# Idle products ahead of the input's transposes, and one query projection moved between the two products of a linear attention

## The chip, the cores and the metric

The kernel runs on one core of a Trainium2 chip. The metric is the device time of one execution in microseconds (us), lower is better. Engines are named as the profile names them: PE is TensorE's matmul side and PEld its weight loads, DVE is VectorE, ACT is ScalarE, POOL is GpSimd, SP is SyncE, whose queue issues most loads.

## The reference

One graph layer over N = 384 nodes with D = 1024 features, everything in float32:

```
xn = layernorm(x)
x  = x + gnn(xn) + mix(xn)
x  = x + moe(layernorm(x))

gnn: q, k, v = xn Wq, xn Wk, xn Wv (+ biases); q2, k2, v2 = q Wiq, k Wik, v Wiv
     16 heads of softmax(q2 k2^T / 8 + edge mask) v2, then Wo
mix: q, k, v = xn Wqkv + b; qp, kp = elu(q) + 1, elu(k) + 1
     attn = qp (kp^T v) / (qp sum(kp) + 1e-6)
     x1 = layernorm(xn + attn); layernorm(x1 + (silu(x1 Wg) * (x1 Wu)) Wd)
moe: 8 experts, each row through the one that its logits pick
```

The change touches the layer norm and transposes at the very start, the linear attention of mix, and the first query projection of gnn.

## The kernel before

The program is written by hand, an instruction stream for each engine, tied by semaphores. Nothing is scheduled by a tool: each engine does its work in the order in which its block of the source has it. Each product in full precision is made of three passes over a high and a low part of both factors (`PASSES`), so every operand has a high half, made by ACT as a rounded copy, and a low half, made by DVE as the difference (`lo`).

**Weights.** They come from one stream of 512 KB quarters. SP loads a quarter into one of four slots of `raw`, ACT rounds it into `wsp` (`prep`, profile line 664), DVE subtracts (`prep`, shown as line 977), and PE takes the quarter (`open_quarter` waits for `w_lo`). The engines stay two quarters ahead. `feature_major` (line 1625) makes one 128-row block of a projection from a quarter: 24 matmuls of 128x384 into PSUM bank 0 or 1, which alternate. `open_acc` makes PE wait until the block before the last has left its bank; `acc_part` (ACT line 671, then DVE line 988) empties a bank into the high and low half of a block of features.

**Start.** SP loads x in three tiles of 128 rows. DVE takes statistics (lines 994 and 996), POOL the reciprocal root (529, 530), DVE scales the tile (1009, `xn_done`). PE transposes each tile in eight blocks (1654), ACT copies them out (679), DVE makes the low half. Then come the quarters of mix's q and k with their elu (lines 695 to 710 on ACT, 1071 on DVE), then v in token order (1639).

**Linear attention.** It is computed as (qp kp^T) v rather than qp (kp^T v). The first product, line 1690, makes three blocks of 384x384 scores from `feat[2]` (keys) and `feat[1]` (queries), evacuated by `acc_part` into `pt`. PE then waits until the last of them is out (`acc_free`), and for each tile of rows makes the denominators (1704, six matmuls of two columns) and the second product (1709, eighteen matmuls of 128x512) into banks 2 to 7. DVE divides, adds and takes statistics for each tile (1134 to 1139).

```
            pe.wait_ge(acc_free, acc.value)
            pe.wait_ge(tm_lo, 2 * NT)
```

**Projections of gnn.** Three loops of two turns with four quarters each follow on PE (line 1715): eight blocks of q into `feat[1]`, eight of k, eight of v. ACT and DVE have matching loops. Between DVE's steps of the query projections stand pieces 12 to 15 of the edge code search (`piece`, line 1053), 10 and 11 stand between the tiles of the linear attention. POOL makes the codes for each piece (lines 556, 558) and then writes edges to DRAM one column at a time (573). SP loads the rows for pieces 10 to 15 between the quarters 24 to 32.

Of the kernel before, what the change touches and what calls it, by code (L numbers as in the profile page):

```python
# [25 lines left out]
P = 128  # L26
# [3 lines left out]
KT = D // P  # L30
# [5 lines left out]
GROUP = 3  # L36
# [10 lines left out]
RING = 4  # L47
# [6 lines left out]
B_MQ, B_MK, B_Q, B_K, B_V, B_IQ, B_IK, B_IV, B_G, B_U = 0, 8, 16, 24, 32, 40, 48, 56, 64, 67  # L54
# [47 lines left out]
@contextmanager  # L102
def repeat(engine, times, per):

    first = {t: t.n for t in per}
    with engine.Fori(0, times) as i:
        for t, n in per.items():
            t.i, t.per = i, n
        yield i
    for t, n in per.items():  # L110
        assert t.n == first[t] + n, (t.n, first[t], n)
        t.n, t.i = first[t] + n * times, None
# [38 lines left out]
def graph_layer(nc, x, rowb, cols, consts, later, src_rows, dst_rows, src_cols, dst_cols, type_cols,  # L151
                type_weights, w_stream, w_experts, switch_w, b12, out):
    with ExitStack() as ctx:
        def sb(name, shape, dt=F32):
            return ctx.enter_context(nc.sbuf_tensor(name, shape, dt))

        def sem(name):
            return ctx.enter_context(nc.semaphore(name))
# [16 lines left out]
        feat = [b[:].rearrange("p h (k n) -> p h k n", k=KT) for b in bigs]  # L175
# [23 lines left out]
        row_buf = sb("row_buf", [P, D])  # L199
# [4 lines left out]
        bias = sb("bias", [P, NBIAS])  # L204
# [6 lines left out]
        with nc.sbuf_tensor("low_rows", [P, N], F32) as low_rows:  # L211
# [42 lines left out]
        junk, late_junk = ([work[:, b * N:(b + 1) * N], work[:, (b + 1) * N:(b + 2) * N - P],  # L254
                            work[:, (b + 2) * N - P:(b + 2) * N]] for b in (2, 4))
# [20 lines left out]
        ps = ctx.enter_context(nc.psum_tensor("ps", [P, 8, HALF], F32))  # L276
# [3 lines left out]
        ys_dram = nc.dram_tensor("slot_y", [SLOTS * SLOT, D], F32).ap()  # L280


        x_in = [sem(f"x_in{t}") for t in range(NT)]
        ident_set, const_in, edge_in, rowb_in, b_row_in, route_in = (
            sem("ident_set"), sem("const_in"), sem("edge_in"), sem("rowb_in"), sem("b_row_in"), sem("route_in"))
# [5 lines left out]
        acc_ready, acc_hi, acc_free = sem("acc_ready"), sem("acc_hi"), sem("acc_free")  # L291
# [360 lines left out]
        def _(act):  # L652
            q_no = Tally()
            used = [Tally() for _ in range(XRING)]
            acc = Tally()
            everyone = slice(0, P)

            def prep(slot):


                act.wait_ge(raw_in[slot], used[slot].add(16))
                if q_no.i is not None or q_no.n >= RING:
                    act.wait_ge(w_started, q_no.value - 1)
                nc.scalar.activation(wsp[:, 0, slot, :], raw[:, slot, :], ACT.Copy).then_inc(w_hi, 1)  # L664
                q_no.add()

            def acc_part(dst, rows, b):

                bank = acc.n % 2
                act.wait_ge(acc_ready, acc.add())  # L670
                nc.scalar.activation(dst, ps[rows, bank, 0:N], ACT.Identity, bias=b).then_inc(acc_hi, 1)  # L671

            turn = {q_no: RING, acc: RING, **{u: 16 for u in used[:RING]}}
# [59 lines left out]
                acc_part(pt[:, 0, mt, :], everyone, 0.0)  # L733


            for n, b0 in enumerate((B_Q, B_K, B_V)):
                with repeat(act, 2, turn) as i:
                    for j in range(RING):
                        m = i * RING + j
                        acc_part(feat[1 + n][:, 0, bass.ds(m, 1), :], everyone, bias[:, bass.ds(m + b0, 1)])  # L740
                        prep((j + 2) % RING)
# [223 lines left out]
        def _(dve):  # L965
            q_no, step = Tally(), Tally()
            acc, hi_no = Tally(), Tally()
            everyone = slice(0, P)
# [10 lines left out]
            def prep(slot):  # L979
                dve.wait_ge(w_hi, q_no.add())  # L980
                lo(wsp[:, 1, slot, :], raw[:, slot, :], wsp[:, 0, slot, :]).then_inc(w_lo, 1)

            def acc_part(dst, hi, rows, b):

                bank = acc.n % 2
                acc.add()
                dve.wait_ge(acc_hi, hi_no.add())
                nc.vector.scalar_tensor_tensor(out=dst, in0=ps[rows, bank, 0:N], scalar=b, in1=hi.bitcast(F32),  # L988
                                               op0=ALU.add, op1=ALU.subtract).then_inc(acc_free, 1)
# [8 lines left out]

            turn = {q_no: RING, acc: RING, hi_no: RING}

            nc.vector.memset(ones_r[:].bitcast(F32), 1.0).then_inc(ones_set, 1)
            for t in range(NT + 1):
                if t < NT:
# [43 lines left out]
            parts, elus, pieces, edges = Tally(), Tally(), Tally(), Tally()  # L1047

            def piece(buf, c, into):

                dve.wait_ge(codes_done, pieces.value + 1)
                for k in range(GROUP):
                    ins = nc.vector.scalar_tensor_tensor(  # L1053
                        out=into[k], in0=codes[buf][:, k * P:N], scalar=ef[:, 0, bass.ds(c + k, 1)],
                        in1=maskb[:, k, k * P:N], op0=ALU.is_equal, op1=ALU.mult,
                        accum_out=dup[:, bass.ds(c + k, 1)])
                ins.then_inc(piece_done, 1)
                dve.wait_ge(piece_done, pieces.add())
                cs = bass.ds(c, GROUP)
                then(nc.vector.scalar_tensor_tensor(out=ef[:, 1, cs], in0=dup[:, cs], scalar=0.0, in1=ef[:, 2, cs],  # L1060
                                                    op0=ALU.is_gt, op1=ALU.mult))
                nc.vector.tensor_tensor(eidx[:, cs], ef[:, 1, cs], ef[:, 0, cs], ALU.add).then_inc(edges_done, 1)
                edges.add()
# [43 lines left out]
            for h in range(2):  # L1107
                for j in range(RING):
                    prep((j + 2) % RING)
                    if j % 2:  # L1110
                        n = 6 + 2 * h + j // 2
# [9 lines left out]
                for t in range(NT):  # L1121
# [2 lines left out]
                    lo(tokv[3][:, 1, t, cols_h], work[:, t * HALF:(t + 1) * HALF], tokv[3][:, 0, t, cols_h])\  # L1124
                        .then_inc(tm_lo, 1)

            for mt in range(NT):
                acc_part(pt[:, 1, mt, :], pt[:, 0, mt, :], everyone, 0.0)


            for t in range(NT):
# [7 lines left out]
                statistics(t)  # L1139
                if t < 2:  # L1140
                    piece(t, (10 + t) * GROUP, late_junk)

            def projection(n, m, j, b0):

                acc_part(feat[1 + n][:, 1, bass.ds(m, 1), :], feat[1 + n][:, 0, bass.ds(m, 1), :],
                         everyone, bias[:, bass.ds(m + b0, 1)])
                prep((j + 2) % RING)

            def x1_scaled(t):

# [9 lines left out]
                nc.vector.scalar_tensor_tensor(out=row, in0=row, scalar=rs[:, t, 1:2], in1=rowbuf[:, 1, :],  # L1160
                                               op0=ALU.mult, op1=ALU.add).then_inc(x1_done, 1)

            with repeat(dve, 2, {**turn, pieces: 2, edges: 2, step: 2}) as i:
                for j in range(RING):
                    projection(0, i * RING + j, j, B_Q)
                    if j % 2:
                        piece(j // 2, i * (2 * GROUP) + (12 + j // 2) * GROUP, late_junk)
            with repeat(dve, 2, turn) as i:
                for j in range(RING):
                    projection(1, i * RING + j, j, B_K)  # L1170
# [431 lines left out]
        def _(pe):  # L1602
            q_no, acc = Tally(), Tally()

            def open_quarter():

                pe.wait_ge(w_lo, q_no.add())
# [9 lines left out]
            def feature_major(slot, moving, between=None, after=3):  # L1617

                open_quarter()
                bank = open_acc()  # L1620
                for k in range(KT):
                    if between and k == after:
                        between()
                    for n, (a, b) in enumerate(PASSES):
                        ins = nc.tensor.matmul(ps[:, bank, 0:N], wsp[:, a, slot, k * P:(k + 1) * P],  # L1625
                                               moving[:, b, k, :], start=(k == 0 and n == 0),
                                               stop=(k == KT - 1 and n == 2))
                        if k == 0 and n == 0:
                            ins.then_inc(w_started, 1)
                ins.then_inc(acc_ready, 1)  # L1630
# [15 lines left out]

            turn = {q_no: RING, acc: RING}

            pe.wait_ge(ident_set, 1)

            for t in range(NT):
                pe.wait_ge(xn_done, t + 1)
                for k in range(KT):
                    ins = nc.tensor.transpose(set_banks(t)[:, k, :], tok[:, t, k * P:(k + 1) * P], ident)
                ins.then_inc(tr_ready, 1)
# [30 lines left out]
            for mt in range(NT):  # L1686
                bank = open_acc()
                for k in range(KT):
                    for n, (a, b) in enumerate(PASSES):
                        ins = nc.tensor.matmul(ps[:, bank, 0:N], feat[2][:, a, k, mt * P:(mt + 1) * P],  # L1690
                                               feat[1][:, b, k, :], start=(k == 0 and n == 0),
                                               stop=(k == KT - 1 and n == 2))
                ins.then_inc(acc_ready, 1)

            pe.wait_ge(acc_free, acc.value)
            pe.wait_ge(tm_lo, 2 * NT)
            pe.wait_ge(ones_set, 1)
            for t in range(NT):
                b0 = 2 + 3 * (t % 2)
                if t == 2:  # L1700
                    pe.wait_ge(num_free, 1)
                for mt in range(NT):
                    for a in range(2):
                        nc.tensor.matmul(ps[:, b0 + 2, 0:2], pt[:, a, mt, t * P:(t + 1) * P], ones_r[:],
                                         start=(mt == 0 and a == 0), stop=(mt == NT - 1 and a == 1))
                for h in range(2):
                    for mt in range(NT):
                        for n, (a, b) in enumerate(PASSES):
                            ins = nc.tensor.matmul(ps[:, b0 + h, :], pt[:, a, mt, t * P:(t + 1) * P],  # L1709
                                                   tokv[3][:, b, mt, h * HALF:(h + 1) * HALF],  # L1710
                                                   start=(mt == 0 and n == 0), stop=(mt == NT - 1 and n == 2))
                ins.then_inc(num_ready, 1)


            for _ in range(3):
                with repeat(pe, 2, turn):
                    for j in range(RING):
                        feature_major(j, feat[0])
# [20 lines left out]
            for t in range(NT):  # L1739
                for h in range(2):  # L1740
                    for k in range(FHT):
# [4 lines left out]
                        for n, (a, b) in enumerate(PASSES):  # L1746
                            ins = nc.tensor.matmul(ps[:, 2 + 2 * t + h, :], pt[:, b, k, t * P:(t + 1) * P],  # L1747
                                                   wsp[:, a, slot, kk * HALF:(kk + 1) * HALF],
                                                   start=(k == 0 and n == 0), stop=(k == FHT - 1 and n == 2))
# [182 lines left out]
            for u in range(2):  # L1932
                both = ps[:, 1, (NT + 2) * EXPERTS:(NT + 4) * EXPERTS].rearrange("p (t e) -> p t e", e=EXPERTS)
                nc.tensor.matmul(both, ones_m, hot_of(u).unsqueeze(1).to_broadcast([P, 2, EXPERTS]),
                                 start=(u == 0), stop=False)
# [143 lines left out]
            with pe.If(over > 0):  # L2079
# [14 lines left out]
                for o in range(OVER):  # L2094
                    pe.wait_ge(place_done, NT + o + 1)
                    for k in range(KT):
                        for part in range(2):
                            for t in range(NT):
                                ins = nc.tensor.matmul(ps[:, 2, k * SLOT:(k + 1) * SLOT], x2_part(part, t, k),
                                                       place_late[:, t, :], start=(t == 0 and part == 0),  # L2100
                                                       stop=(t == NT - 1 and part == 1))
# [95 lines left out]
```

## Time and profile before

| | |
|---|---|
| median of 3 runs | 583.62 us |
| the runs | 584.11, 581.46, 583.62 us |
| profiled execution | 583.34 us, span 581.6 us |
| busy PE, PEld, DVE, ACT, POOL | 95, 82, 65, 41, 25% of the span |
| chain that ended last | PE 82%, DVE 10%, ACT 3% |
| mean granted clock of TensorE | 0.991 |

The profiled execution is one run, recorded by the hardware; its time is 1.74 us longer than the span from its first to its last instruction. All starts below are counted from the span's start. The chain that ended last is followed back from the last instruction to whatever released each step; time of an engine on that chain is time the kernel would be shorter without. The granted clock is the share of TensorE's full 2.4 GHz that the records show.

### The profile page before, as it was taken

What the parts mean: (1) busy time and instruction counts of PE and PEld (TensorE: products, weight loads), DVE (VectorE), ACT (ScalarE), POOL (GpSimd) and SP (SyncE); (2) the same over time, 40 slices, a digit from 0 to 9 for tenths busy, and PEclk for the clock granted to TensorE, in tenths of its full rate; (3) what the DMA queues carried; (4) which work ended last, traced back from release to release, by engine and by line L of the source; (5) the groups of instructions that cost most, each with busy time, mean ns of one, the idle gap of its engine ahead of it and who ended that gap; (6) DMA issues with size and microseconds to landing.
All of it is one profiled execution on the core that took longest, in us unless ns stands there. A gap on an engine that the chain in (4) does not pass through costs nothing.

```text
span 581.6 us, 8599 instructions
## 1 busy us (share of the span) xinstructions
PE 554.0 (95%) x3087; PEld 475.6 (82%) x3087; DVE 380.7 (65%) x747; ACT 240.1 (41%) x392; POOL 146.1 (25%) x161
## 2 busy tenths in 40 slices
PE   3989999999999999999999999999998998999996
PEld 2889998897999999999978999999997886733342
DVE  6678887953777436774448898889889886300115
ACT  4645554320233333344317647665676514320000
POOL 5626766660266510062000000001002011000020
PEclk9989999999999999999999999999999998999999
DMA  8656657550164463338633234426339879099963
GB/s 307 213 141 163 181 162 207 176 144 1 45 181 140 143 213 125 127 127 280 172 109 108 73 109 108 109 73 161 127 115 332 285 289 346 21 386 409 411 233 113
DMA packets 33778, 104.19 MB, mean 179 GB/s; under 512 B 5424, under 2 KB 9712, under 8 KB 33744
## 3 DMA queue, kind: packets, MB, share of 16 engines
q1 hardware_dynamic: 28224, 89.95, 45.1%
q0 software_dynamic: 5376, 13.29, 8.8%
q10 hardware_dynamic: 144, 0.52, 0.3%
q8 instruction: 18, 0.29, 0.2%
q14 instruction: 16, 0.13, 0.1%
HBM read 96.58 MB, written 5.60 MB: 176 GB/s over the span
## 4 chain that ended last, share of the span: by engine, by line
PE 82%; DVE 10%; ACT 3%; issue 2%; DMA 1%; DVEq 0%; POOL 0%; SPq 0%; ACTq 0%
PE ps L1625 42%; PE ps L1976 9%; PE ps L1639 6%; PE ps L1818 5%; DVE wsp L977 3%; PE ps L1772 3%; PE ps L1762 3%; PE ps L1922 2%; PE ps L1747 2%; PE ps L1709 2%; PE ps L1690 2%; PE ps L1782 2%; PE ps L2024 1%; DMA tok<-in_x 1%; DVE big L977 1%
## 5 line engine op out<-in xcount | busy, mean ns | idle before, releaser
L1625 PE MATMUL ps<-big,wsp 128*128 128x384 f32 x1656 | 297.7, 338 | 4.5 <-DVE wsp L977 3.2
L1625 PEld LDWEIGHTS ps<-big,wsp 128*128 128x128 f32 x1656 | 287.6, 189 | 9.5 <-issue 5.3
L977 DVE TENSOR_TENSOR wsp<-raw,wsp 128x1024 fp32r<-128x1024 f32 x85 | 111.8, 1320 | 30.7 <-ACT wsp L664 29.7
L664 ACT ACTIVATE wsp<-raw 128x1024 fp32r<-128x1024 f32 x83 | 86.9, 1052 | 32.7 <-PE ps L1639 12.9
L573 POOL DMA_INDIRECT edge_table<-ef,eidx x48 | 55.3, 1152 | 35.7 <-DMA edge_table<-ef,eidx 22.4
L671 ACT ACTIVATE big<-ps,bias 128x384 f32 x24 | 14.0, 583 | 80.9 <-PE ps L1625 80.9
L988 DVE SCALAR_TENSOR_TENSOR big<-ps,bias,big 128x384 f32 (+1 forms) x24 | 14.8, 618 | 34.1 <-ACT big L671 33.5
L1976 PE MATMUL ps<-blocks 128*64 128x512 f32 x160 | 36.5, 598 | 0.1
L788 ACT ACTIVATE work<-work,snm 128x384 f32<-128x384 f32 x48 | 28.9, 605 | 16.1 <-DVE snm L1244 16.1
L1639 PE MATMUL ps<-wsp,big 128*128 128x512 f32 x144 | 33.0, 390 | 0.0
L1639 PEld LDWEIGHTS ps<-wsp,big 128*128 128x128 f32 x144 | 26.9, 188 | 5.8 <-DVE wsp L977 0.3
L610 POOL DMA_DIRECT2D tok<-rowbuf x3 | 2.8, 935 | 96.7 <-ACT tok L815 96.7
L1976 PEld LDWEIGHTS ps<-blocks 128*64 128x64 f32 x160 | 10.6, 136 | 19.6 <-issue 19.0
L529 POOL TENSOR_SCALAR rs<-mv 128x1 f32<-128x1 f32 x12 | 6.1, 506 | 80.2 <-DVE mv L996 47.3
L1240 DVE CUSTOM_DVE_ANT_0 work<-ps,maskb 128x384 f32<-128x384 f32 x48 | 24.1, 553 | 1.6 <-issue 1.6
L1532 DVE COPY maskb<-ps 128x512 f32<-128x512 f32 x4 | 2.8, 692 | 33.7 <-PE ps L1976 33.7
L977 DVE TENSOR_TENSOR pt<-ps,pt 128x1152 fp32r<-128x1152 f32 x16 | 21.7, 1357 | 1.3 <-ACT pt L796 1.3
L1053 DVE SCALAR_TENSOR_TENSOR work<-codes,ef,maskb 128x384 f32<-128x384 int32 (+2 forms) x48 | 22.1, 509 | 0.0
L1772 PE MATMUL ps<-pt,vp 128*128 128x384 f32 x96 | 20.1, 344 | 1.0 <-DVE pt L977 0.7
L1250 DVE TENSOR_SCALAR work<-work,sinv 128x384 f32<-128x384 f32 x48 | 19.1, 455 | 0.6
L796 ACT ACTIVATE pt<-ps 128x1152 fp32r<-128x1152 f32 x16 | 18.1, 1134 | 3.1 <-PE ps L1762 3.0
L1762 PE MATMUL ps<-cst,work 128*128 128x128 f32 x144 | 18.6, 274 | 0.9 <-DVE work L1250 0.9
(259 smaller groups left out, 704.8 us busy)
## 6 DMA issues: line engine op xcount, KB each, us to landing
raw<-in_w_stream SPq DMA_DIRECT2D x85, 512.0 KB, 3.7
blocks<-in_w_experts SPq DMA_DIRECT2D x64, 512.0 KB, 8.9
rowbuf<-in_rowb POOLq DMA_DIRECT2D x6, 512.0 KB, 6.3
raw_x<-in_w_stream SPq DMA_DIRECT2D x4, 512.0 KB, 7.4
slot_y<-rowbuf POOLq DMA_DIRECT2D x7, 256.0 KB, 5.7
tok<-in_x SPq DMA_DIRECT2D x3, 512.0 KB, 4.2
edges_a<-in_src_rows SPq DMA_DIRECT2D x8, 192.0 KB, 4.0
edges_a<-in_dst_rows SPq DMA_DIRECT2D x8, 192.0 KB, 5.4
```

The lines of the kernel that those rows point to most:

```text
L573: pool.indirect_dma_start(out=table, out_offset=bass.IndirectOffsetOnAxis(ap=eidx[:, c:c + 1], axis=0), in_=ef[:, 3, c:c + 1], in_offset=N ...
L664: nc.scalar.activation(wsp[:, 0, slot, :], raw[:, slot, :], ACT.Copy).then_inc(w_hi, 1)
L788: nc.scalar.activation(probs[:, s, t, :], probs[:, s, t, :], ACT.Exp, bias=snm[:, s, t:t + 1], scale=DH ** -0.5, accum_out=ssum[:, s, t:t ...
L977: return nc.vector.tensor_tensor(dst, value, hi.bitcast(F32), ALU.subtract)
L1053: ins = nc.vector.scalar_tensor_tensor(out=into[k], in0=codes[buf][:, k * P:N], scalar=ef[:, 0, bass.ds(c + k, 1)], in1=maskb[:, k, k * P: ...
L1240: ins = nc.vector.tensor_tensor_reduce(out=probs[:, s, t, :], in0=ps[:, 2 + 3 * s + t, 0:N], in1=maskb[:, t, :], scale=1.0, scalar=3.0 * N ...
L1625: ins = nc.tensor.matmul(ps[:, bank, 0:N], wsp[:, a, slot, k * P:(k + 1) * P], moving[:, b, k, :], start=(k == 0 and n == 0), stop=(k == K ...
L1639: ins = nc.tensor.matmul(ps[:, banks + t, :], stationary[:, b, k, t * P:(t + 1) * P], wsp[:, a, slot, kk * HALF:(kk + 1) * HALF], start=(k ...
L1762: ins = nc.tensor.transpose(ps[:, b + mt, t * P:(t + 1) * P], probs[:, s, t, mt * P:(mt + 1) * P], ident)
L1772: ins = nc.tensor.matmul(ps[:, bank, 0:N], vp[:, mt, s, :], pt[:, b, mt, :], start=(mt == 0 and b == 0), stop=(mt == NT - 1 and b == 1))
L1818: ins = nc.tensor.matmul(ps[:, 2 + 3 * h + t, :], feat[0][:, b, k, t * P:(t + 1) * P], split_of(slot_of(Q_WO + h * RING + j), a)[:, kk * H ...
L1976: ins = nc.tensor.matmul(ps[s * SLOT:(s + 1) * SLOT, bank, :], stationary(k, s), rows[s][:, kk * HALF:(kk + 1) * HALF], start=False, stop= ...
```

## The change

Two places. At the start DVE first clears 256 columns of `row_buf`, and PE multiplies this cleared block with itself: 14 products of 128x128 in plain float32 ahead of the first tile's transposes, 3 ahead of the second tile's and 1 ahead of the third's. They write a part of bank 1 that nothing reads. Nothing else of the start moves.

In the linear attention the first of the eight query projections (quarter 24) is taken after the three score blocks and ahead of the wait for their last evacuation. The wait's value is kept from before the projection. ACT and DVE empty the projection's bank right behind the third score block, and prepare quarter 26 there. The other seven query projections are written out on PE, ACT and DVE instead of looped; the pieces of the edge search stay behind the second, fourth, sixth and eighth block.

```diff
+        warm_set = sem("warm_set")
@@ ACT
-            for n, b0 in enumerate((B_Q, B_K, B_V)):
+            for m in range(KT):
+                acc_part(feat[1][:, 0, m, :], everyone, bias[:, B_Q + m:B_Q + m + 1])
+                prep((m + 2) % RING)
+            for n, b0 in enumerate((B_K, B_V), 1):
@@ DVE
+            nc.vector.memset(row_buf[:, 0:2 * P], 0.0).then_inc(warm_set, 1)
             nc.vector.memset(ones_r[:].bitcast(F32), 1.0).then_inc(ones_set, 1)
@@
             for mt in range(NT):
                 acc_part(pt[:, 1, mt, :], pt[:, 0, mt, :], everyone, 0.0)
+            projection(0, 0, 0, B_Q)
@@
-            with repeat(dve, 2, {**turn, pieces: 2, edges: 2, step: 2}) as i:
-                for j in range(RING):
-                    projection(0, i * RING + j, j, B_Q)
-                    if j % 2:
-                        piece(j // 2, i * (2 * GROUP) + (12 + j // 2) * GROUP, late_junk)
+            for m in range(1, KT):
+                projection(0, m, m % RING, B_Q)
+                if m % 2:
+                    piece(m // 2 % 2, (12 + m // 2) * GROUP, late_junk)
@@ PE
+            def warm(times):
+
+                for _ in range(times):
+                    nc.tensor.matmul(ps[:, 1, 0:P], row_buf[:, 0:P], row_buf[:, P:2 * P], start=True, stop=True)
+
+            pe.wait_ge(warm_set, 1)
+            warm(14)
             pe.wait_ge(ident_set, 1)
 
             for t in range(NT):
+                if t:
+                    warm(5 - 2 * t)
                 pe.wait_ge(xn_done, t + 1)
@@
-            pe.wait_ge(acc_free, acc.value)
+            scores_acc = acc.value
+            feature_major(0, feat[0])
+            pe.wait_ge(acc_free, scores_acc)
             pe.wait_ge(tm_lo, 2 * NT)
@@
-            for _ in range(3):
+            for m in range(1, KT):
+                feature_major(m % RING, feat[0])
+            for _ in range(2):
```

PE between the products of the linear attention, before (big1 and big2 are queries and keys of mix, big3 its values, big0 the transposed input):

```order
L1690 MATMUL ps<-big1,big2 128x384 x72
L1704 MATMUL ps<-ones_r,pt 128x2 x6
L1709 MATMUL ps<-big3,pt 128x512 x18
L1704 MATMUL ps<-ones_r,pt 128x2 x6
L1709 MATMUL ps<-big3,pt 128x512 x18
L1704 MATMUL ps<-ones_r,pt 128x2 x6
L1709 MATMUL ps<-big3,pt 128x512 x18
```

and with the change:

```order
L1704 MATMUL ps<-big1,big2 128x384 x72
L1630 MATMUL ps<-big0,wsp 128x384 x24
L1720 MATMUL ps<-ones_r,pt 128x2 x6
L1725 MATMUL ps<-big3,pt 128x512 x18
L1720 MATMUL ps<-ones_r,pt 128x2 x6
L1725 MATMUL ps<-big3,pt 128x512 x18
L1720 MATMUL ps<-ones_r,pt 128x2 x6
L1725 MATMUL ps<-big3,pt 128x512 x18
L1630 MATMUL ps<-big0,wsp 128x384 x168
```

The 24 matmuls of one projection stand between the score blocks and the denominators; seven projections, 168 matmuls, follow the second product without a branch.

DVE at the same place with the change:

```order
L992 SCALAR_TENSOR_TENSOR pt<-ps,pt 128x384 x3
L992 SCALAR_TENSOR_TENSOR big<-ps,bias,big 128x384
L981 TENSOR_TENSOR wsp<-raw,wsp 128x1024
L1146 TENSOR_SCALAR den<-ps 128x1
L1147 RECIPROCAL den<-den 128x1
L1148 SCALAR_TENSOR_TENSOR tok<-ps,den,tok 128x1024
```

The second and third row are new there: the low half of the projected block and of quarter 26. Before, they stood first behind the third tile's statistics.

## Rows read from the trace of the kernel before

**Rows 1.** The page: its first line, and the chain's shares by engine.
```profile
span 581.6 us, 8599 instructions
...
PE 82%; DVE 10%; ACT 3%; issue 2%; DMA 1%; DVEq 0%; POOL 0%; SPq 0%; ACTq 0%
```

**Rows 2.** The chain that ended last, start (us), length (us), what; first 23 us.
```profile
10.92 0.81 DVE tok L1009
...
12.87 3.40 DVE big L977 x3
16.26 4.02 DVE wsp L977 x3
20.28 0.40 DVE tw L1020
...
21.02 0.57 ACT work L695
```

**Rows 3.** The timeline of the start: start, length, engine, line, operation, idle before.
```profile
0.88 0.06 DVE L1001 MEMSET ones_r<- 128x2 f32 x1 [0.88 <-PEq L2190]
...
7.94 1.57 PEld L1654 LDWEIGHTS ps<-cst,tok 128*128 128x128 f32 x8 [7.94 <-issue]
...
7.97 1.94 PE L1654 MATMUL ps<-cst,tok 128*128 128x128 f32 x8 [7.97 <-DVE tok L1009]
...
10.21 2.68 PE L1654 MATMUL ps<-cst,tok 128*128 128x128 f32 x16 [0.29 <-DVE tok L1009]
...
11.78 0.86 PEld L1654 LDWEIGHTS ps<-cst,tok 128*128 128x128 f32 x8 [0.22 <-DVE tok L1009]
...
14.09 4.42 PE L1660 MATMUL ps<-big,wsp 128*128 128x384 f32 x24 [1.20 <-ACT big L679]
```

**Rows 4.** Groups of PE's matmuls by shape: busy us, mean ns, idle before.
```profile
L2059 PE MATMUL ps<-row_buf,iota 128*128 128x512 f32 x12 | 5.4, 601 | 0.0
```

**Rows 5.** The chain, transposes of x1, which run long after the start.
```profile
250.23 2.62 PE ps L1725 x24
```

**Rows 6.** PE in stretches: from:to, length, busy (instructions), granted clock, DMA share, GB/s.
```profile
33.00:34.00 1.00, 0.00 (x0) 1.00 0.00 0
...
36.00:37.00 1.00, 1.00 (x4) 0.50 0.99 377
```

**Rows 7.** The chain at 34.69 us, 24 matmuls of one quarter.
```profile
34.69 6.04 PE ps L1625 x24
```

**Rows 8.** The chain through the linear attention and the first projections.
```profile
133.93 0.50 ACT pt L671
...
134.45 0.57 DVE pt L988
...
135.06 0.83 PE ps L1704 x6
135.89 4.23 PE ps L1709 x18
140.12 0.56 PE ps L1704 x6
140.68 4.21 PE ps L1709 x18
...
149.67 24.99 PE ps L1625 x144
...
174.76 8.59 PE ps L1625 x48
```

**Rows 9.** The timeline of DVE during the query projections.
```profile
155.60 1.23 DVE L977 TENSOR_TENSOR wsp<-raw,wsp 128x1024 fp32r<-128x1024 f32 x1
...
160.95 0.61 DVE L1053 SCALAR_TENSOR_TENSOR work<-codes,ef,maskb 128x384 f32<-128x384 int32 x1
...
169.70 1.37 DVE L1053 SCALAR_TENSOR_TENSOR work<-codes,ef,maskb 128x384 f32<-128x384 int32 x1
...
176.45 2.23 DVE L977 TENSOR_TENSOR wsp<-raw,wsp 128x1024 fp32r<-128x1024 f32 x1
```

More of the change, by code:

```diff
@@ L1125, in _, with projection @@
                         .then_inc(tm_lo, 1)
+            def projection(n, m, j, b0):
+                acc_part(feat[1 + n][:, 1, bass.ds(m, 1), :], feat[1 + n][:, 0, bass.ds(m, 1), :],
+                         everyone, bias[:, bass.ds(m + b0, 1)])
+                prep((j + 2) % RING)
             for mt in range(NT):
                 acc_part(pt[:, 1, mt, :], pt[:, 0, mt, :], everyone, 0.0)
+            projection(0, 0, 0, B_Q)
             for t in range(NT):
@@ L1141, in _ @@
                     piece(t, (10 + t) * GROUP, late_junk)
[L1143 to L1147, printed above, removed]
             def x1_scaled(t):
```

## The prediction

> **What bounds the kernel.** I read the page first: PE is 82% of the chain that ended last, DVE 10% [rows 1]. So a microsecond in which PE stands still is worth a microsecond wherever the chain runs over PE, and nothing where it runs over another engine. The change touches two stretches, and the chain's own rows tell which kind each is. In the first 23 us it runs over DVE without a gap: scaling of the third tile, the low half of a weight quarter, three low halves of the transposed input, three more quarters, the edge weights' first step, and only then the first elu on ACT at 21.02 [rows 2]. No transpose is in it. From the linear attention to 250 us it is PE alone, but for one interruption: a rounded copy on ACT and a difference on DVE between score block three and the first denominator [rows 8]. These are the two places to price.
>
> **Sum or state.** Time is counted against the profiled execution, 583.34 us, which is 0.28 below the median of the three runs, 583.62. The runs themselves lie 2.65 us apart, and a measurement can tell about 0.5% (2.9 us) from no change.
>
> **The start.** What is added: a memset of 256 columns on DVE, before statistics for which it waits on the load of x anyway: nothing. Then 14 + 3 + 1 products on PE. What bounds their price: the six products of line 2059 show as 12 records of 5.4 us together, so 0.90 us for 512 columns and, by columns, 0.225 for 128 [rows 4]. That is at the upper of the clock's two levels, 2.4 GHz. At the lower one, 1.2 GHz, I double it: 0.45. The first transposes take 1.94 us for eight [rows 3], 0.24 each, where the transposes of x1 take 2.62 us for 24, 0.11 each [rows 5]; so PE starts the kernel at the lower level, although nothing of that is in the granted clock column there. Fourteen products are 3.2 to 6.3 us. They begin behind DVE's memsets, at about 1.1 us [rows 3], and end at 4.3 to 7.4 us, before the 7.97 at which the first tile is ready. They delay nothing.
>
> What they can save: with the clock up, eight transposes take 0.87 instead of 1.94, and their weight loads 0.86 as the third group has already, instead of 1.57 [rows 3]. That is some 1.0 us of the first group, up to 0.7 of the second, nothing of the third. All of it lies beside DVE's chain. The third group is already fast, so PE's first quarter at 14.09 moves by at most 0.1 us; and its result is wanted by ACT only at 21.02, though it is there at about 18.5 [rows 2, 3]. There are 2.5 us of slack. I take **0** for the start. The ends: no gain beyond 0, since no row of the chain there is PE's; a loss if the clock stays down: then three products of 0.45 lie behind a group that ends at 9.91 and push the second group from 10.21 to 11.26, the single product and the slower third group push that from 11.78 to 13.5 and its end to 15.4, ACT's third copy ends at 16.5, and DVE, which would begin the third low half at 15.1 (two thirds through the 3.40 of 12.87), waits 1.4 us. So the start is 0 to +1.4.
>
> The Trainium skill, "TensorE: Matmul & The Clock Gate", Part 4, says that transposes do not bring the clock up because they don't count as work of the array. Here the third group's loads take 0.86 us for eight against 1.57 for the first [rows 3], with nothing but transposes before them, so the trace disagrees. By the page the third group too would gain, and the sum would still be 0, as it is DVE's.
>
> **The linear attention.** Before: the chain leaves PE at 133.90, spends 0.50 on ACT and 0.57 on DVE, comes back at 135.06, and the six small products take 0.83, so that the second product begins at 135.89 [rows 8]: 1.99 us behind the end of the scores. Between tiles the same six products take 0.56 [rows 8]. With the projection in between, the 1.07 us of evacuation lies under 4.17 us of projection (24.99 for 144 matmuls is six of them), and 0.56 is left. Gain: 1.99 - 0.56 = **1.43 us**. Can the projection start at once? Its quarter, 24, is one of the two that are always ahead; its bank was filled by the second score block and emptied while the third ran. Both yes.
>
> What moves along: the second product and DVE's divisions come 4.17 - 1.43 = 2.7 us later, which only the pieces 10 and 11 and, on POOL, their edges feel; POOL has no part in the chain. SP: quarter 30's load waits for quarter 26 to be split, now at about 141 (133.9 + 4.17, and 2 to 3 us for ACT and DVE) instead of 157 [rows 9], so this load and the rows of piece 13 behind it go out 16 us earlier. The loads of 31 and 32 with pieces 14 and 15 keep their place behind the second and third query projection.
>
> Behind the second product seven projections follow instead of eight. In the eight of before, six ran at 4.17 and two took 8.59, 0.25 us over [rows 8]: there DVE was late with a low half. DVE's piece took 1.37 instead of 0.61 for its first step beside POOL's making of codes, and a low half of a quarter 2.23 instead of 1.23 [rows 9]. With piece 13's rows there early, POOL's work spreads differently and that 0.25 may go or come back. I take 0; the ends are -0.25 and what the second rival gives. Loops written out: the page shows no loss of PE at their branches, 0.
>
> **The sum.** 583.34 + 0 - 1.43 = 581.9 for an execution like the profiled one; added to the median, 583.62 - 1.43 = 582.2. I forecast **582.2 us**, 0.25% less.
>
> **Rivals.**
>
> *The clock's fall does not come.* At 33 us PE stands still [rows 6]; soon after it resumes, the granted clock is 0.50, and the quarter of 34.69 takes 6.04 us instead of 4.17 [rows 6 to 8]: 1.87 us lost on the chain. An earlier fall or none would be chance; the run of 581.46 is 1.9 below the profiled one, and may be one without it. If the median execution after the change lacks it: 582.2 - 1.9 = 580.3. For it: the spread. Against: nothing in the change makes PE's gap at 33 shorter, as PE waits for ACT and DVE there. A fifth.
>
> *DVE is late in the query projections; slower.* DVE prepares a quarter 1.2 us before PE opens it: the low half of 155.60 is done at 156.83, and the third quarter opens at 149.67 + 8.33 = 158.0 [rows 8, 9]. Beside POOL that work is longer by 1.0 for the low half and 0.76 for a piece's first step [rows 9], 1.76 together. It decides from 1.2 us on: if all four pieces meet POOL, PE waits 0.56 at each, 2.2 us. Should ACT's evacuation be caught by it as well, the piece's whole lateness of 0.76 may come on top once. Then 582.2 + 2.2 + 0.8 = 585.2. For it: the one lapse of before was of this sort. Against: now POOL has its rows earlier. One in ten.
>
> *A second fall, or the products at the lower clock.* The idle products end up to 3.7 us before the first tile comes, and the clock could be down again; or a second gap of PE while ACT and DVE hold the chain brings a second fall. By the first the start costs up to 1.4, by the second 1.9: 583.6 to 584.1. The Trainium skill, "TensorE: Matmul & The Clock Gate", section "HAM oscillation", says that a wait for data between bursts of matmuls puts the clock back down, which speaks against idle products that stop early; the fall at 35 us agrees. It changes the transposes' speed, not the chain. One in ten.
>
> *The change does not do what it says.* The stall moves: the denominators wait for something else, or the seven projections lose at their start what was gained. Then 583.6. One in twenty.
>
> **How the numbers follow.** 0.55 for the forecast (581.6 to 582.6, as the last 0.25 falls), 0.2, 0.1, 0.1, 0.05 for the rivals. Faster by over 0.5% means under 580.7: the first rival alone, 0.2. Slower by over 0.5% means over 586.5: the tail of the second, 0.04. Rest 0.76. The range takes in the first and third rival and leaves out the second: 580.0 to 584.1.
>
> **What would show it.** Right: in the chain no ACT or DVE row between the score blocks and the second product, the first denominators at 0.56 us, the second product ahead of the seventh to eighth projection, the last query projection ended 1.4 to 1.7 us earlier than 183.4. In the start, transposes of 0.11 us from the first on, and yet DVE's rows from 10.92 to 21 where they are. Wrong: a PE wait for a low half of `wsp` of over 0.3 us between 150 and 185, an ACT copy of the transposes in the chain, or the fall of the clock at another place or absent. If the elu at 21.02 moves earlier by over 0.3 us, my reading of the start is wrong.

## The result, and the profile after

The changed kernel takes 579.28 us, median of 6 runs (578.03 to 580.58), against 583.70 for the kernel before (6 runs, 581.46 to 584.11). The ratio is 0.9932, 95% interval 0.9914 to 0.995: 4.0 us shorter, and by the interval 2.9 to 5.0 (the two medians alone lie 4.4 apart). I had forecast 1.43 us shorter, 582.2 us in a range of 580.0 to 584.1.

| | before | after |
|---|---|---|
| profiled execution, its span | 583.34, 581.6 us | 578.34, 576.6 us |
| busy PE, DVE | 95, 65% | 96, 66% |
| chain: PE, DVE, ACT | 82, 10, 3% | 82, 11, 3% |
| mean granted clock | 0.991 | 0.996 |

The chain of the changed kernel's start, to be held against [rows 2] (start, length, what):

```profile
10.61 0.81 DVE tok L1014
...
12.56 3.40 DVE big L981 x3
15.96 4.02 DVE wsp L981 x3
...
20.71 0.57 ACT work L696
```

It is the same chain with the same lengths. It begins 0.31 us sooner, because x's third tile came sooner, and nothing in it got shorter. The timeline shows that the idle products (line 1657) did what they are meant to do to PE, as against [rows 3]:

```profile
1.25 5.52 PE L1657 MATMUL ps<-row_buf 128*128 128x128 f32 x28 [1.25 <-DVE row_buf L1005]
...
7.88 1.06 PE L1668 MATMUL ps<-cst,tok 128*128 128x128 f32 x8 [1.10 <-DVE tok L1014]
...
13.78 4.43 PE L1674 MATMUL ps<-big,wsp 128*128 128x384 f32 x24 [1.21 <-ACT big L680]
```

Fourteen products are 28 records and end at 6.8 us, inside the 4.3 to 7.4 of the forecast. The first tile's transposes take 1.06 us instead of 1.94. PE's first quarter still begins as far ahead of its place before (0.31) as the tile was.

The chain through the linear attention, against [rows 8]:

```profile
119.97 12.50 PE ps L1704 x72
132.47 4.16 PE ps L1630 x24
136.63 0.56 PE ps L1720 x6
137.20 4.20 PE ps L1725 x18
...
150.94 39.22 PE ps L1630 x225
```

No ACT or DVE row interrupts it any more. To see where the time went I compare landmarks: the start of the same work in the two profiles, changed kernel less kernel before. These are the scaling of the third tile -0.31; the scores (121.38 and 119.97) -1.41; the end of the second product (149.67 with 4.17 for the projection now behind it, and 150.94) -2.90; the transposes of x1 (250.23 and 246.85) -3.38; PE's last product (570.65 and 565.94) -4.71. Of that the linear attention is 1.49, as forecast. The other parts were not forecast: 1.10 ahead of it, 0.48 in the projections and 1.33 behind them. The fall of the clock at 35 us is absent here. The kernel before has a second fall, at 489 us, which the prediction did not count; it is absent too, and the changed kernel has one at 442 us instead. The second of these rows is of the kernel before, the other two of the changed one:

```profile
34.70:36.00 1.30, 1.30 (x9) 1.00 0.59 123
...
490.00:500.00 10.00, 9.54 (x44) 0.70 0.50 203
...
444.00:446.00 2.00, 2.00 (x6) 0.50 1.02 418
```

(Stretch, length, PE busy with its instructions in brackets, granted clock, DMA share, GB/s.) So two questions: how much of the gain is luck with the clock, and what else there is.

### The profile page after: what moved, and what is told of

It is laid out like the page before. It is cut to its first block, busy times and chain, and to the rows that moved or that the text cites. A ratio compares the mean times of both kernels' runs of the same rounds, so it can differ in the third digit from the quotient of the medians.

```text
span 576.6 us, 8563 instructions
## 1 busy us (share of the span) xinstructions
PE 555.4 (96%) x3123; PEld 478.4 (83%) x3123; DVE 382.4 (66%) x748; ACT 240.1 (42%) x392; POOL 146.1 (25%) x161
## 4 chain that ended last, share of the span: by engine, by line
PE 82%; DVE 11%; ACT 3%; issue 2%; DMA 1%; POOL 0%; DVEq 0%; ACTq 0%
PE ps L1630 42%; PE ps L1994 9%; PE ps L1836 6%; PE ps L1644 5%; DVE wsp L981 3%; PE ps L1790 3%; PE ps L1780 3%; PE ps L1765 2%; PE ps L1725 2%; PE ps L1704 2%; PE ps L1800 2%; PE ps L1940 2%; PE ps L2042 1%; DVE big L981 1%; ACT wsp L665 1%
## 5 line engine op out<-in xcount | busy, mean ns | idle before, releaser
L981 DVE TENSOR_TENSOR wsp<-raw,wsp 128x1024 fp32r<-128x1024 f32 x85 | 110.4, 1303 | 31.8 <-ACT wsp L665 31.1
L672 ACT ACTIVATE big<-ps,bias 128x384 f32 (+1 forms) x24 | 14.0, 583 | 78.9 <-PE ps L1630 78.9
L992 DVE SCALAR_TENSOR_TENSOR big<-ps,bias,big 128x384 fp32r<-128x384 f32 (+1 forms) x24 | 14.8, 618 | 35.3 <-ACT big L672 35.3
L1644 PE MATMUL ps<-wsp,big 128*128 128x512 f32 x144 | 33.1, 390 | 0.5 <-DVE wsp L981 0.5
L1836 PE MATMUL ps<-wsp,big 128*128 128x512 f32 x72 | 18.9, 420 | 1.8 <-DVE snm L1249 1.8
L1058 DVE SCALAR_TENSOR_TENSOR work<-codes,ef,maskb 128x384 f32<-128x384 int32 (+2 forms) x48 | 20.6, 479 | 0.0
```

Of the source, the lines that this page charges most:

```text
L981: return nc.vector.tensor_tensor(dst, value, hi.bitcast(F32), ALU.subtract)
L1058: ins = nc.vector.scalar_tensor_tensor(out=into[k], in0=codes[buf][:, k * P:N], scalar=ef[:, 0, bass.ds(c + k, 1)], in1=maskb[:, k, k * P: ...
L1644: ins = nc.tensor.matmul(ps[:, banks + t, :], stationary[:, b, k, t * P:(t + 1) * P], wsp[:, a, slot, kk * HALF:(kk + 1) * HALF], start=(k ...
L1836: ins = nc.tensor.matmul(ps[:, 2 + 3 * h + t, :], feat[0][:, b, k, t * P:(t + 1) * P], split_of(slot_of(Q_WO + h * RING + j), a)[:, kk * H ...
```

## The experiments

**One part at a time.** The first four kernels are the kernel before again (e0), the 18 idle products alone (e1), the moved block with the written-out ones but without idle products (e2), and the written-out blocks alone, none moved (e3). The last one is this edit on PE, with ACT and DVE alike (one file against the other; nothing else differs):

```diff
-            for _ in range(3):
+            for m in range(KT):
+                feature_major(m % RING, feat[0])
+            for _ in range(2):
                 with repeat(pe, 2, turn):
```

> The kernel before, unchanged, so that each run's granted clock is seen. Theory A (part of the 4.4 us is chance of the clock): runs differ by up to 3 us, the short ones with a clock near 1.000 and the long ones near 0.991, ratio 1.000. Theory B (the idle products keep the clock up): every run has a clock of 0.992 or less, ratio 1.000.

> Only the 18 idle products and the memset of the change. Theory A: the start's chain is DVE's, so the time is that of before, within 0.7 us, and the elu behind the first quarter stays at 20.7 to 21.1 us. Theory B: the clock falls less often than in the unchanged kernel, and the time is 1.5 to 2.5 us shorter, with a mean clock over 0.994.

> Only the moved projection and the seven that are written out; no idle products. Theory A: 2 us shorter than before (1.5 in the linear attention, 0.5 in the query projections), apart from the clock's falls. Theory B: 2 us shorter and falls of the clock as in the kernel before, so 1.5 to 2.5 us longer than the full change.

> Only the eight query projections written out instead of looped, none moved. Theory A: 0 to 0.5 us shorter: the query projections lose 0.2 us to DVE in the loop. Rival theory C (the written-out code is a good part of the gain, as DVE's pieces need no register steps): 1 us or more shorter.

| kernel | median (runs) | lowest to highest | ratio to before, 95% |
|---|---|---|---|
| before again | 583.75 (11) | 581.94 to 586.14 | 1.0024, 1.0007 to 1.0042 |
| idle products at the start alone | 583.57 (12) | 581.94 to 586.53 | 1.0018, 0.9999 to 1.0038 |
| moved and written out | 579.27 (6) | 578.45 to 580.44 | 0.9948, 0.9931 to 0.9964 |
| written out alone | 582.42 (12) | 579.61 to 583.43 | 0.998, 0.996 to 1.0001 |

The same kernel against itself comes out at 1.0024 with an interval that leaves out 1: differences under 0.3% are not to be trusted here. Its longest runs (585.74 to 586.14) have a mean granted clock of 0.982 or 0.983, its shortest (581.94) one of 0.994, as theory A has it. The idle products at the start alone gain nothing (1.0018). The gain comes with the second edit: without idle products the ratio is 0.9948 (0.9931 to 0.9964), the whole change had 0.9932 (0.9914 to 0.995), and the intervals overlap. Theory B has fallen. Theory A expected 2 us from e2, which has 3.0 by its ratio, and 0 to 0.5 us from e3, which has 0.5 by the medians and 1.2 by its ratio, too close to the noise to choose between A and C.

Writing out alone shows in the chain of e3, against [rows 8]:

```profile
147.91 99.87 PE ps L1627 x576
```

24 quarters in one piece, 4.161 each. The kernel before needs 100.56 from 149.67 to 250.23 for the same 24, its repetition 100.84 (149.66 to 250.50), the kernel with idle products at the start 100.90. So up to that point the loops cost 0.7 to 1.0 us. The repetition shows one part of it (chain, same columns):

```profile
149.66 16.68 PE ps L1625 x96
...
169.97 2.06 DVE work L1053 x6
...
173.68 1.23 DVE wsp L977
175.03 8.61 PE ps L1625 x48
```

DVE reaches its piece late, with rows of DVE's own queue ahead of each step (in the loop the steps take their addresses from registers), then its low half of the next quarter is late, and PE waits: the quarters of 149.66 should have ended at 174.63 (six of 4.161), and the next begins at 175.03. That is 0.40 of this profile's 0.97. Counted from the first query quarter, PE wants this low half after 24.97 us, and DVE ends it after 24.96 in the kernel before, 25.24 in the repetition and 24.10 in e3. The rest is spread over the next two quarters and the two loops behind, about 0.28 each, with no wait that the profile names. Which engine's loop costs what is not shown, since e3 writes out all three.

Between the profiles of e3 and e2 the moved block alone is worth 247.78 - 246.43 = 1.35 at x1's transposes, and 1.47 with e2's scores standing 0.12 later. Yet the medians lie 3.15 us apart, so 1.7 us remained beyond the moved block's own gain. The record of the runs points at the clock: the mean granted clock is 0.9894 over the twelve runs of e3 and 0.9937 over the six of e2.

**The clock's falls filled.** In all profiles so far the falls followed PE's gaps at 33 us, at 442 us and in the routing work from 485 us on. I put idle products of the identity into these, in four kernels (the cut shows the added lines; `@@` says where they stand):

```diff
+            def fill(times, bank):
+                for _ in range(times):
+                    nc.tensor.matmul(ps[:, bank, N:HALF], ident, ident, start=True, stop=True)
@@ after the first four quarters
+            fill(6, 7)
@@ before the first quarter of Wo
+            pe.wait_ge(acc_free, acc.value)
+            fill(6, 0)
@@ around the transposes of x2's last tile, and before the last logits
+            fill(2, 3)
+            fill(1, 3)
+            fill(1, 3)
```

> The kernel before, with idle products of the identity in PE's gaps at 33, 442 and 485 us, six, six and four of them, so that the clock has less reason to fall there. Theory A (what is left of the gain beside the moved block and the written-out code is the clock's falls, which come by chance at these three gaps): a narrower spread, about 581.3 us, near the shortest runs of the kernel before. Rival D (a third mechanism of the change, nothing to do with the clock): the products move nothing, 583 us with the old spread.

> Query projections written out in place, and the same fillers. Theory A: 0.7 to 1.0 us below the filled kernel before, about 580.5. Rival D: 582.4 as without fillers.

> The moved block with the written-out ones, without the idle products at the start, and the same fillers. Theory A: 1.4 to 1.5 us below the filled kernel with the written-out blocks alone, about 579.0. Rival D: 2.5 us or more below it.

> The whole change and the same fillers: theory A and D both put it with the filled kernel without the idle products at the start, within 0.5 us, as these products did nothing; a rival by which the front counts only where nothing else falls: 1 us below it.

| filled kernel | median (runs) | lowest to highest | ratio to before, 95% |
|---|---|---|---|
| before | 580.81 (6) | 579.30 to 581.73 | 0.995, 0.9935 to 0.9965 |
| written out | 579.55 (6) | 579.08 to 581.30 | 0.9939, 0.9923 to 0.9955 |
| moved and written out | 577.74 (4) | 577.52 to 579.05 | 0.9897, 0.9882 to 0.9911 |
| the whole change | 577.50 (4) | 577.25 to 578.02 | 0.9896, 0.9882 to 0.9911 |

Every kernel gets shorter, so the falls at these gaps do cost time: 2.9 us of the kernel before, and 1.8 of the change against its own earlier runs. Rival D has fallen: it expected no effect. Theory A's sizes hold roughly: writing out is worth 1.3 us by the medians (0.7 to 1.0 expected), the move 1.8 (1.4 to 1.5 expected), and idle products at the start 0.2 (none expected). The filled profiles of before, of written out and of the whole change have no fall between 30 and 530 us. Their x1 transposes stand at 248.62, 247.95 and 246.28. With the scores at 119.56, 119.83 and 119.60 taken off, writing out is worth 0.94 at this point and the move 1.44.

The whole executions, 579.67, 579.29 and 577.37 us, give the same total (2.30 against 2.38) but divide it otherwise: 0.38 for writing out and 1.92 for the move. In this pair part of what writing out gained is lost again at one later wait of PE for DVE, first the kernel before, then the written-out one:

```profile
447.57 1.18 PE L1768 MATMUL ps<-cst,work 128*128 128x128 f32 x9 [0.34 <-DVE work L1250]
447.50 1.17 PE L1772 MATMUL ps<-cst,work 128*128 128x128 f32 x9 [0.84 <-DVE work L1252]
```

The 0.67 by which x1's transposes came sooner has shrunk to 0.07 here. So writing out is worth 0.94 where it acts, and at the end of the kernel it varies: two more pairs of single executions without a fall, each on one chip, lie 0.98 (g3 and g4 below) and 1.42 us apart (h4 and h1).

Written-out code and move together are thus worth 2.3 to 2.4 us. The medians of the filled kernels differ by 3.3. The spread hints at why: the filled kernels with the gap in the linear attention have runs 1.8 us and more above their shortest (581.13, 581.24, 581.73 of six, from 579.30 on; 581.25, 581.30 of six, from 579.08 on). Those with the moved block reach 1.5 us at most: 579.05 of f2, from 577.52 on. This one was profiled, and it has a fall in the routing work from 488 us on, where the fillers leave short gaps (waits of 0.2 and 0.3 us):

```profile
480.00:490.00 10.00, 9.06 (x86) 0.90 0.97 373
490.00:500.00 10.00, 10.00 (x45) 0.93 0.16 65
```

So the fillers make falls rarer and do not rule them out.

**The gap in the linear attention.** Theory E: there is a fourth gap where the clock can fall, and it is the one that the moved block closes. A further filler stands where the block would (g1 has it, g2 is the written-out filled kernel again, unchanged):

```diff
-            pe.wait_ge(acc_free, acc.value)
             pe.wait_ge(tm_lo, 2 * NT)
+            fill(4, 7)
+            pe.wait_ge(acc_free, acc.value)
```

> The written-out blocks with the fillers at 33, 442 and 485 us, and four more idle products in the gap between the two products of the linear attention. Theory E (that gap of 1.17 us, with small products behind it, is a fourth place where the clock falls in some executions; the moved block closes it): no run over 580.5, all at 579.0 to 579.8; the gap itself stays, as evacuation takes as long. Rival F (the upper runs of the filled kernels come from somewhere else): still a third to a half of the runs at 581.0 to 581.7.

> The same without the four: control on the same chip. Both theories: a third to a half of the runs at 581.0 to 581.7, the rest at 579.0 to 579.8.

> The kernel before with fillers, one look, for a profile of an upper run. Theory E: if its time is near 581.3, the granted clock falls between 135 and 150 us and nowhere else. Rival F: it falls elsewhere, or the clock is 1.00 all through.

> The written-out blocks with fillers, one look for the same purpose: theory E, if its time is near 581.2, the granted clock falls between 135 and 150 us; rival F, elsewhere.

With the gap filled (g1): 579.16, 579.20, 579.34, 579.49, 580.09, 580.35. Without (g2), on the same chip: 578.75, 578.93, 579.32, 579.77, 580.90, 580.97, 581.10, 581.23. The group at 580.9 and above is gone. The two at 580.09 and 580.35 were not expected; they have no profile. PE's timeline shows that nothing else changed, since the products fit into the gap:

```profile
132.07 1.05 PE L1654 MATMUL ps<-cst 128*128 128x128 f32 x8
133.40 0.83 PE L1713 MATMUL ps<-ones_r,pt 128*128 128x2 f32 x6 [0.28 <-DVE pt L991]
```

The idle time before the denominators is 0.28 instead of 1.17, and they begin where they began. Six runs against eight are few, so I take all timed filled runs together, each held against the shortest of its own kernel: with the gap open nine of 20 are 1.8 us or more above it, with the gap closed (by the block or by products) none of 14, the highest being 1.53 above. Seven of the nine have a mean granted clock of 0.996; no run with the gap closed is below 0.997. The two single executions g3 and g4, at 579.94 and 578.96 us, had no fall, so four more were profiled.

> Look at the filled kernel with written-out blocks. Theory E: a run of 580.8 to 581.3 us shows the granted clock down at the second product, between 134 and 145 us, and the second product's 18 matmuls there take up to 8 us instead of 4.2. Rival F: an upper run shows the fall elsewhere.

> Look at the filled kernel before. Theory E: an upper run, near 581.3 us, has its fall at the second product of the linear attention. Rival F: elsewhere.

> As h1, to catch an upper run. Theory E: an upper run falls at 134 to 145 us. Rival F: elsewhere.

> As h2, to catch an upper run. Theory E: an upper run falls at 134 to 145 us. Rival F: elsewhere.

They came at 578.89, 581.29, 580.55 and 580.31 us, h1 to h4. Two of them, h2 and h3, have a fall, and it is at this gap and nowhere else before 570 us. The filled kernel before at 581.29, PE in stretches, and its chain:

```profile
134.00:136.00 2.00, 2.00 (x9) 0.79 0.03 8
136.00:138.00 2.00, 2.00 (x7) 0.50 0.00 0
```

```profile
134.22 5.81 PE ps L1715 x18
...
140.59 4.21 PE ps L1715 x18
```

The first tile of the second product takes 5.81 us, the second 4.21 (I had expected up to 8 for the first). The other one, written out, at 580.55:

```profile
134.00:136.00 2.00, 2.00 (x7) 0.56 0.04 8
```

```profile
134.06 5.82 PE ps L1717 x18
```

In h1, the same kernel at 578.89, this tile takes 4.19:

```profile
134.16 4.19 PE ps L1717 x18
```

The fall costs 5.82 - 4.19 = 1.63 us between these two executions of one kernel. PE being the chain there, nothing gives it back up to x1's transposes: with the scores taken off they stand 1.63 later, and the times lie 1.66 apart. Theory E holds: the clock can fall at this gap. That every long run is one of these does not follow, as f2's fall shows. (The Trainium skill, "TensorE: Matmul & The Clock Gate", section "HAM oscillation", has the clock fall when a wait for data parts two bursts of matmuls. h2 and h3 agree that a fall follows a pause between bursts; this pause, 1.17 us, is much shorter than the waits in the page's example, and it is ACT and DVE that PE waits for, not a load.)

h4, the filled kernel before at 580.31 with a mean clock of 0.998, has no fall. Against the filled kernel before at 579.67 its scores stand 0.35 later and the work at 454 us 0.74 later (454.68 against 453.94), in small pieces. One of f0's runs, at 580.50, has a mean clock of 1.000. So times of this kernel up to 580.5 need no fall, and the time alone does not always tell which run has one.

## Why the prediction was wrong

**What bounds the kernel**: right. The start's chain is DVE's, and no idle product could shorten it: the idle products alone measure 1.0018, and in the changed kernel the elu's 20.71 is the tile's 0.31 and nothing more. The transposes' own speed changed as forecast and was worth 0.

**The stall, 1.99 - 0.56 = 1.43**: right. 1.49 between before and after, 1.44 between the filled kernels, 1.47 between e2 and e3.

**"Loops written out: the page shows no loss of PE at their branches, 0", and the 0.25 of DVE's lateness taken as 0**: this term was mis-sized, and it is the step whose failure the profiles show directly. It measured 0.7 to 1.0 us up to x1's transposes, and 0.4 to 1.4 at the end of the kernel in three pairs of executions without a fall, 0.9 on average. I had looked at the eight query projections alone, and at one of the two things in them, the meeting of DVE with POOL. I had written that the 0.25 "may go or come back", where I should have compared all 24 quarters with 24 times the best one: 100.56 against 99.87. Some 0.3 of the loss is in the two loops behind (66.84 to 66.85 us for 16 quarters against 66.57), which the edit doesn't touch. Why these too run without loss when the loop before them is gone, no run tells.

**"A second fall" and "The clock's fall does not come"**: here the mechanism was the right one and the place was missed, which is the second step that failed. I priced falls of the clock at the gap at 33 us, as luck that the change cannot touch: "nothing in the change makes PE's gap at 33 shorter". Two things escaped me. The kernel before has a second fall in the same profile, from 489 us on. And the change removes a gap, the one at 134 us, which I counted at its own length only. In the filled kernels seven (by clock) to nine (by time) of 20 runs look like ones with a fall there, at 1.62 us each, which makes another 0.6 to 0.7 us on average. (Of the nine profiles of filled kernels with this gap two have the fall, which would be 0.4 us.) That it is as much in the kernels without fillers is not shown: none of the four profiles of unfilled kernels with that gap has the fall there. The low clock at 35 us [rows 6, 7] was the hint that gaps have a second price.

**The sum as the runs have it**: 1.45 for the stall, 0.7 to 1.0 for the written-out code, 0.4 to 0.7 for the fall that can no longer come, this last an estimate: 2.6 to 3.2 us. e2 measured 3.0 us (0.9948), the filled change against the filled before 3.3 by medians. The 4.0 of the changed kernel's own runs has an interval from 2.9 to 5.0, so some 0.8 to 1.4 us of it stay open. The granted clock says of what kind they are: its mean is 0.9955 over the six runs of the change, 0.9937 over those of e2, and 0.9889 over 28 runs of the kernel before, where h2 and h3, with one fall of 1.6 us, have 0.996 against 0.999 and 1.000 for the same kernels without. So the unfilled kernels with the moved block have at least one fall less per execution, going by the clock, which is more than the gap at 134 us accounts for. Whether the other gaps bring fewer falls because the work stands elsewhere in time, or by chance of a few runs, no run tells.

**The rivals**: the late DVE had it the wrong way around; it was the loop, not the written-out code, in which DVE came late. The forecast's first rival, 580.3 us without the fall at 35 us, came true in the profiled execution as luck, and is still 1.0 above the measured median. The range of 580.0 to 584.1 left out the case in which the small terms count together.

## What to carry to other kernels

A gap of PE on the chain costs its length and, in some executions, a fall of the clock behind it, which here costs more (1.6 us) than the gap itself (1.2 us). Look at every gap of a microsecond or more and move work that is already ready into it; where there is none, idle products cost nothing here as long as they ended before the wait did: sixteen of them, at 33, 442 and 485 us, took 2.9 us from the kernel before and, in the changed kernel, gave the best version of this study, 577.50 us against 583.69 (0.9896). They are worth nothing where another engine holds the chain, as at this kernel's start. And price a loop against the best iteration over its whole length before calling its overhead zero. But a gain on PE reaches the end of the kernel only where no other engine takes over the chain later: in one pair of profiles more than half of the 0.94 us did not.

## What the runs showed of the hardware

- A gap of only 1.17 us, with six two-column products behind it, was followed by a granted clock of 0.50 (1.2 GHz) in two of the nine profiles of filled kernels that have this gap (f0, f1, g2, g3, g4 and h1 to h4); by clock and time seven to nine of 20 timed runs look the same. In other executions of the same program the clock stayed. After 2.15 us without work at 33 us it fell in three of the six profiles of unfilled kernels. What decides between executions of one program, no run shows.
- The granted clock column reads 1.00 in the kernel before at 8 us, while the transposes there run at half the speed of those at 250 us (0.24 against 0.11 us each). The column did not show the lower clock at the start of the kernel.
- A plain float32 product of 128x128 is two records; 28 records took 5.52 us from 1.25 us on in the changed kernel, the rise of the clock included, and six took 0.83 with the clock up.
